# Half-row sections of an attention kernel's TensorE stream also hold the queries' last products and half of the diagonal key tile

## The reference, cut to what matters

```python
q_nop = (c_Q @ Wq_up)            # 16 heads x 128
q_pe  = rope(c_Q @ Wq_pe)        # 16 heads x 64
scores = einsum(q, k) * SCALE    # q = [q_nop, q_pe], k = [k_nop, k_pe]
scores = where(tril, scores, min)
attn = softmax(scores); y = attn @ v; out = y @ Wo
```

## Time and profile before

| what | value |
|---|---|
| median of 3 runs | 1749.84 us (1749.19 to 1750.82) |
| the profiled execution, own time | 1748.17 us |
| its span in the trace | 1746.1 us |
| TensorE clock granted, mean | 0.992 of full speed |
| attention starts (first of the units' stream) | 106.0 us |
| PE, DVE, ACT, POOL busy | 97%, 76%, 65%, 33% of the span |

### The profile page before, as it was taken

How to read it: one execution, slowest core, us unless ns; L and a number is a source line. 1 busy time by engine, 2 the same in 40 slices (tenths; PEclk the granted TensorE clock), 3 DMA queues, 4 the chain that set the end, 5 groups by cost and what they waited for, 6 DMA issues and landing times.

```text
span 1746.1 us, 29372 instructions
## 1 busy us (share of the span) xinstructions
PE 1688.8 (97%) x9224; PEld 852.3 (49%) x9224; DVE 1332.8 (76%) x3370; ACT 1135.1 (65%) x2464; POOL 583.5 (33%) x1042
## 2 busy tenths in 40 slices
PE   4589999999999999999999999999999999999999
PEld 3345545454544545544454455555454454554444
DVE  5688787777778787787868788777878878777775
ACT  5677666666666666666667566666766666666663
POOL 1223333333333333433333333333333333333330
PEclk9899999999999999999999999999999999999999
DMA  9338977878979787886879978887797888897786
GB/s 267 83 70 146 152 138 146 147 143 153 153 129 151 152 148 149 154 154 123 154 135 155 173 136 148 143 148 132 150 159 141 154 145 147 150 152 145 138 152 129
DMA packets 911877, 255.05 MB, mean 146 GB/s; under 512 B 897384, under 2 KB 899946, under 8 KB 911338
## 3 DMA queue, kind: packets, MB, share of 16 engines
q1 hardware_dynamic: 902336, 235.29, 75.7%
q10 hardware_dynamic: 8938, 15.80, 3.1%
q0 software_dynamic: 448, 2.10, 0.5%
HBM read 20.32 MB, written 8.39 MB: 16 GB/s over the span
## 4 chain that ended last, share of the span: by engine, by line
PE 85%; DVE 4%; issue 4%; ACT 3%; DMA 2%; POOL 1%; SPq 1%; ACTq 0%; DVEq 0%; POOLq 0%
PE bank L623 7%; PE bank L591 7%; PE bank L593 7%; PE bank L594 7%; PE bank L592 7%; PE bank L625 6%; PE bank L624 6%; PE bank L657 6%; PE bank L659 6%; PE bank L658 6%; PE bank L603 3%; DMA XT<-XS 2%; PE bank L596 2%; PE bank L397 2%; PE bank L398 1%
## 5 line engine op out<-in xcount | busy, mean ns | idle before, releaser
L924 ACT ACTIVATE P<-P,nm 128x512 f32<-128x512 f32 (+7 forms) x512 | 395.0, 772 | 459.6 <-DVE nm L1332 457.6
L1332 DVE CUSTOM_DVE_ANT_0 P<-bank,mask,neg 128x512 f32<-128x512 f32 (+7 forms) x512 | 402.5, 814 | 280.2 <-PE bank L603 167.7
L1554 POOL TENSOR_SCALAR sn<-sm 128x1 f32<-128x1 f32 x512 | 206.8, 405 | 944.8 <-ACT P L924 935.1
L919 ACT ACTIVATE F<-P,rc 128x512 f16<-128x512 f32 (+7 forms) x512 | 384.8, 767 | 85.2 <-DVE rc L1340 65.4
L1346 DVE SCALAR_TENSOR_TENSOR F<-P,rc,F 128x512 f16<-128x512 f32 (+7 forms) x512 | 413.3, 819 | 2.8 <-ACT F L919 2.4
L592 PE MATMUL bank<-K,Q 128*128 128x512 f16 (+3 forms) x760 | 248.5, 327 | 0.0
L594 PE MATMUL bank<-K,Q 128*128 128x512 f16 (+3 forms) x760 | 248.5, 327 | 0.0
L591 PE MATMUL bank<-K,Q 128*128 128x512 f16 (+3 forms) x760 | 248.5, 327 | 0.0
L593 PE MATMUL bank<-K,Q 128*128 128x512 f16 (+3 forms) x760 | 248.5, 327 | 0.0
L623 PE MATMUL bank<-FT,V 128*128 128x512 f16 x568 | 216.7, 382 | 3.3 <-DVE WO L1381 3.3
L624 PE MATMUL bank<-FT,V 128*128 128x512 f16 x568 | 215.5, 379 | 0.0
(11 more groups left out here) (211 smaller groups left out, 2675.8 us busy)
## 6 DMA issues: line engine op xcount, KB each, us to landing
out<-X ACTq DMA_DIRECT2D x31, 256.0 KB, 3.5
X<-in_x ACTq DMA_DIRECT2D x28, 256.0 KB, 3.6
FT<-F SPq DMA_TRANSPOSE x348, 4.2
wo<-in_Wo SPq DMA_DIRECT2D x4, 1024.0 KB, 9.0
V<-CC SPq DMA_DIRECT2D x32, 64.0 KB, 2.4
Q<-QS SPq DMA_TRANSPOSE x128, 4.0
X<-in_x SPq DMA_DIRECT2D x4, 256.0 KB, 7.4
ua<-in_Wq_up SPq DMA_DIRECT2D x1, 1024.0 KB, 8.6
```

What stands on the lines that cost most here:

```text
L919: return e.eng.activation(dst, src, ACT.Copy, scale=scale)
L924: e.eng.activation(m.P[:, u % 4, 0:w], m.P[:, u % 4, 0:w], ACT.Exp, bias=m.nm[:, u % 8:u % 8 + 1], scale=-1.0, accum_out=m.sm[:, u % 8:u % ...
L1332: e.eng.tensor_tensor_reduce(out=m.P[:, u % 4, 0:w], in0=m.pS[u % 2][:, off:off + w], in1=m.mask[:, 1024 - w:1024], scale=m.neg[:, :], sca ...
```

## The change

`sections(n)` gives two truth values for unit n: whether the half-row section of quarter 0 and that of quarter 2 are widened. The second is true for all n below 124; the first where the tile of unit n + 2 has i >= 2 besides, and n is not `late`. `halved(n, p)` now says for each pair of heads whether its fifth products are done in halves: for i >= 4 as before (that test is now called `wide`), and for every pair that stands ahead of a widened section, so also for i below 4.

Quarter 0, where widened: behind the two half-row score products comes `up_pe_half(n + 4)`, rows 64 to 127 of `lb` against the high weights, 256 columns, then `diagonal_half`: for the diagonal key tile, queries 0 to 63 of each head against keys 0 to 63 alone (rows 0 to 63), high x high, 256 columns; then `diagonal_rest`, queries 64 to 127 against all 128 keys, in all rows, 256 columns. Keys 64 to 127 are masked for queries 0 to 63, so that nothing is left out there.

Quarter 2, where widened: `up_half(n + 4)`, 512 columns in rows 64 to 127; `diagonal_half` for the other two products of the diagonal, 2 x 256 columns in rows 0 to 63; `diagonal_rest` for these, 2 x 256 columns in all rows. If the unit's quarter 0 was not widened, the diagonal's high x high product follows whole (512 columns).

So `up` and `up_pe` have four full products left instead of five, and `weigh` runs over j = 0 to i - 1 alone, cut anew into quarters (k = i instead of i + 1). For i = 0 no weighing is left outside quarter 2. The waits move along: those of `up_pe` and `up` to ahead of the half products, that of the first weighing (`weigh_ready`) to the first part of the diagonal where quarter 0 is widened or i = 0. The weights' halves change places (high parts in rows 64 to 127), the copies that write them keep their shapes. The half products leave out low x low of the 64 channels.

The diff, cut to its core (`up_pe` and `up_pe_half` are changed as `up` and `up_half` are; the remaining lines exchange the halves of the weights or rename `halved` to `wide`):

```diff
@@ -52,9 +52,22 @@
     JBASE.append(JBASE[-1] + where(_n)[1] + 1)
 
 
+def sections(n):
+
+
+
+    both = n + 2 * AHEAD < N
+    return both and where(n + AHEAD)[1] >= 2 and not late(n), both
+
+
+def halved(n, p):
+
+    return wide(where(n)[1]) or sections(n - AHEAD)[p]
+
+
 def quarter(n, q):
 
-    k = where(n)[1] + 1
+    k = where(n)[1] + (not sections(n)[1])
     return range(-(-k * q // 4), -(-k * (q + 1) // 4))
 
 
...
@@ -406,23 +419,34 @@
     def __init__(self, e, m, s):
         self.e, self.m, self.s = e, m, s
 
-    def up(self, n):
-        e, m, s = self.e, self.m, self.s
-        t, g = divmod(n, NG)
+    def up_ready(self, n):
+        e, s = self.e, self.s
         if n >= NG:
             e.wait_ge(s.ropeq, n + 1)
         elif n:
             e.wait_ge(s.ql, n)
+
+    def up_half(self, n):
+
+        m, (t, g) = self.m, divmod(n, NG)
+        self.up_ready(n)
+        self.e.eng.matmul(m.pU, m.C[64:128, t % 2, 3, :], m.WM[64:128, g, WMB:WMB + 512], start=True, stop=False)
+
+    def up(self, n, begun=False):
+        e, m, s = self.e, self.m, self.s
+        t, g = divmod(n, NG)
+        self.up_ready(n)
         W = m.WM[:, g, :]
         hq, hb, lq, lb = (m.C[:, t % 2, k, :] for k in range(4))
-        e.eng.matmul(m.pU, hq, W[:, WMA:WMA + 512], start=True, stop=False)
+        e.eng.matmul(m.pU, hq, W[:, WMA:WMA + 512], start=not begun, stop=False)
+        if not begun:
+            e.eng.matmul(m.pU, lb, W[:, WMB:WMB + 512], start=False, stop=False)
         e.eng.matmul(m.pU, hq, W[:, WMA + 512:WMA + 1024], start=False, stop=False)
         e.eng.matmul(m.pU, lq, W[:, WMA:WMA + 512], start=False, stop=False)
-        e.eng.matmul(m.pU, hb, W[:, WMB:WMB + 512], start=False, stop=False)
-        e.eng.matmul(m.pU, lb, W[:, WMB:WMB + 512], start=False, stop=True).then_inc(s.up, 1)
-
-    def up_pe(self, n):
-        e, m, s = self.e, self.m, self.s
+        e.eng.matmul(m.pU, hb, W[:, WMB:WMB + 512], start=False, stop=True).then_inc(s.up, 1)
+
+    def up_pe_ready(self, n):
+        e, s = self.e, self.s
         t, g = divmod(n, NG)
         e.wait_ge(s.c_in, 16 * (t + 1))
         e.wait_ge(s.wpl, 2 * min(n + 1, NG))
...
@@ -592,11 +629,11 @@
                 e.eng.matmul(o, Q[:, h, :], K[:, ALO, keys], start=False, stop=False)
                 e.eng.matmul(o, Q[:, 4 + h, :], K[:, AHI, keys], start=False, stop=False)
                 e.eng.matmul(o, Q[:, 8 + h, :], K[:, BHI, keys], start=False, stop=False)
-                if not halved(i):
+                if not halved(n, p):
                     op = e.eng.matmul(o, Q[:, 8 + h, :], K[:, BLO, keys], start=False, stop=True)
-            if not halved(i):
+            if not halved(n, p):
                 op.then_inc(s.s, 1)
-        if halved(i):
+        if halved(n, p):
             for lo, hi in cuts:
                 for h, top in ((2 * p, 0), (2 * p + 1, 64)):
                     o, keys = m.pS[h % 2][:, off + lo:off + hi], slice(base + lo, base + hi)
@@ -604,25 +641,64 @@
                     if hi == cuts[-1][1]:
                         op.then_inc(s.s, 1)
 
-    def weigh(n, j):
-        b, i, g = where(n)
+    downs = ffns = 0
+
+    def weigh_ready(n):
+
         for z in range(GROUP_OF[4 * n], GROUP_OF[4 * n + 3] + 1):
             e.wait_ge(s.ft_in[z % FSLOTS], 16 * (z // FSLOTS + 1))
         e.wait_ge(s.v_in, 16 * (n // NG + 1))
         if n >= 2:
             e.wait_ge(s.yl, n - 1)
-        if j == 0 and n:
-            e.wait_ge(s.cr, tiles.downs)
-            e.wait_ge(s.od, tiles.ffns)
-        elif j == 0:
+        if n:
+            e.wait_ge(s.cr, downs)
+            e.wait_ge(s.od, ffns)
+        else:
             e.wait_ge(s.wol, 16)
+
+    def weighed(n, j, lo, hi):
+
+
+        b, i, g = where(n)
         ft = turned_at(m, n, 0, 1024 * (i + 1)).rearrange("p (h c q) -> p h c q", h=4, q=128)
-        hi, lo = ft[:, :, j, :], ft[:, :, i + 1 + j, :]
-        o = m.pY[n % 2].rearrange("p (h q) -> p h q", h=4)
         V = m.V[:, key_slot(b, j), :, :]
-        e.eng.matmul(o, V[:, 0, :], hi, start=(j == 0), stop=False)
-        e.eng.matmul(o, V[:, 0, :], lo, start=False, stop=False)
-        e.eng.matmul(o, V[:, 1, :], hi, start=False, stop=(j == i)).then_inc(s.pv, 1)
+        o = m.pY[n % 2].rearrange("p (h q) -> p h q", h=4)[:, :, lo:hi]
+        return o, V[:, 0, :], V[:, 1, :], ft[:, :, j, lo:hi], ft[:, :, i + 1 + j, lo:hi]
+
+    def weigh(n, j, start=False, stop=False):
+        o, vh, vl, hi, lo = weighed(n, j, 0, 128)
+        if start:
+            weigh_ready(n)
+        e.eng.matmul(o, vh, hi, start=start, stop=False)
+        e.eng.matmul(o, vh, lo, start=False, stop=False)
+        e.eng.matmul(o, vl, hi, start=False, stop=stop).then_inc(s.pv, 1)
+
+    def diagonal_half(n, first, start=False):
+
+
+        o, vh, vl, hi, lo = weighed(n, where(n)[1], 0, 64)
+        if start:
+            weigh_ready(n)
+        if first:
+            e.eng.matmul(o, vh[0:64], hi[0:64], start=start, stop=False)
+        else:
+            e.eng.matmul(o, vh[0:64], lo[0:64], start=start, stop=False)
+            e.eng.matmul(o, vl[0:64], hi[0:64], start=False, stop=False)
+
+    def diagonal_rest(n, first, stop=False):
+
+        o, vh, vl, hi, lo = weighed(n, where(n)[1], 64, 128)
+        if first:
+            op = e.eng.matmul(o, vh, hi, start=False, stop=stop)
+        else:
+            e.eng.matmul(o, vh, lo, start=False, stop=False)
+            op = e.eng.matmul(o, vl, hi, start=False, stop=stop)
+        return op
+
+    def diagonal_whole(n, stop=False):
+
+        o, vh, vl, hi, lo = weighed(n, where(n)[1], 0, 128)
+        return e.eng.matmul(o, vh, hi, start=False, stop=stop)
 
     def weigh_pair(p):
 
@@ -669,24 +745,41 @@
             tiles.down(2, m.pO)
     for n in range(N - 1):
         t, g = divmod(n, NG)
+        first, second = sections(n)
+        k = where(n)[1] + (not second)
+        done = 0
+        downs, ffns = tiles.downs, tiles.ffns
         for q in range(4):
             if q % 2 == 0 and n + AHEAD < N:
                 pair(n + AHEAD, q // 2)
+            if q == 0 and first:
+                queries.up_pe_half(n + 2 * AHEAD)
+                diagonal_half(n, True, start=True)
+                diagonal_rest(n, True)
             if q == 0 and late(n):
                 queries.up_pe(n + 2 * AHEAD)
                 combine(n - 1, 0)
+            if q == 2 and second:
+                queries.up_half(n + 2 * AHEAD)
+                diagonal_half(n, False, not first and done == 0)
+                op = diagonal_rest(n, False, first and done == k)
+                if not first:
+                    op = diagonal_whole(n, done == k)
+                op.then_inc(s.pv, 1)
             for j in quarter(n, q):
-                weigh(n, j)
+                done += 1
+                weigh(n, j, not first and j == 0, done == k and (q >= 2 or not second))
             if q == 0 and n + 2 * AHEAD < N and not late(n):
-                queries.up_pe(n + 2 * AHEAD)
+                queries.up_pe(n + 2 * AHEAD, first)
             if q == 1 and (g == 3 and t + LEAD < T or g == 0 and t + LEAD - 1 < T):
                 e.wait_ge(s.yl, n)
+                e.wait_ge(s.wol, 16)
                 if g:
                     tiles.down(t + LEAD, m.pY[(n + 1) % 2])
                 else:
                     tiles.ffn(t + LEAD - 1, m.pY[(n + 1) % 2])
             if q == 2 and n + 2 * AHEAD < N:
-                queries.up(n + 2 * AHEAD)
+                queries.up(n + 2 * AHEAD, second)
             if q % 2 and n and n + AHEAD < N and not (q == 1 and late(n)):
                 combine(n - 1, q // 2)
     combine(N - 3, 0)
...
@@ -831,17 +924,17 @@
         e.wait_ge(s.wm, 2 * k + 1)
         copy(W[:, WMA:WMA + 512], fold_bank(m, k, 3), m.sq[:, 0:1]).then_inc(s.wph, 1)
         e.wait_ge(s.wm, 2 * k + 2)
-        copy(W[0:64, WMB:WMB + 512], fold_bank(m, k, 4)[0:64, :], m.sq[0:64, 1:2]).then_inc(s.wph, 1)
+        copy(W[64:128, WMB:WMB + 512], fold_bank(m, k, 4)[64:128, :], m.sq[64:128, 1:2]).then_inc(s.wph, 1)
         if k:
             e.wait_ge(s.wpl, 2 * k)
-        copy(m.tmp[64:128, :], fold_bank(m, k, 4)[64:128, :], m.sq[64:128, 1:2]).then_inc(s.wph, 1)
+        copy(m.tmp[0:64, :], fold_bank(m, k, 4)[0:64, :], m.sq[0:64, 1:2]).then_inc(s.wph, 1)
 
     def rotary_out():
         e.wait_ge(s.ld_pb, 32)
         e.wait_ge(s.sc, 1)
         copy(m.WM[:, :, WQA:WQA + 256], m.pa[:, :, :], m.sqp[:, 0:1]).then_inc(s.wrh, 1)
-        copy(m.WM[0:64, :, WQB:WQB + 256], m.pbw[0:64, :, :], m.sqp[0:64, 1:2]).then_inc(s.wrh, 1)
```

More of the change, by code:

```diff
@@ L108, in score_cuts, with wide @@
     return off, [(0, cut)] + ([(cut, w)] if w > cut else [])
-def halved(i):
+def wide(i):
     return i >= 4
 def early(n):
-    return halved(where(n)[1]) and (n == N - 1 or not halved(where(n + 1)[1]))
+    return wide(where(n)[1]) and (n == N - 1 or not wide(where(n + 1)[1]))
 def late(n):
@@ L435, in up_pe, with up_pe_half @@
```

(32 more changed lines are left out.)

## The result

The changed kernel runs in 1737.94 us (median of 4 runs, 1737.78 to 1739.36), the kernel before in 1750.06 (4 runs, 1749.19 to 1750.82): ratio 0.9933, 95% interval 0.9915 to 0.995. Forecast were 1740.8 us and 9.0 us less; it became 12.1 less (by the interval 8.8 to 14.9 us, which holds the forecast).

The account below looks back on a forecast made before the run. PE, busy 97%, was taken as the bound, with only 0.28 us to spare before waiting for DVE. 30.0 us saved less 21.0 given back left 9.0: 1749.84 - 9.0 = 1740.8 us, range 1728 to 1756.

Parts of the forecast that it names:

- other such places: Unspecified places like the one between index 5 and 0, where PE may wait: 1.5 us given back.
- PE's side: Slots saved on PE: 8.8 us in quarter 0, 25.3 in quarter 2, less 4.1 for new low-index sections; 30.0 in all.
- fixed 0.20 of a section: Each half-row section on PE costs 0.20 us once: 0.09 to enter, 0.09 to leave, 0.01 a pair.
- new sections in low tiles: Pairs of heads with index below 4 get a half-row section they lacked: 4.1 us lost on PE in sum.
- Unequal halves: Quarter 2: forecast took full overlap; the rival said no overlap as pairs, 13.6 us back, 1754.4, slower, chance 0.12.
- Waits behind late masks: PE waits for YL behind later masks; index 2: combine at 4.30 us, waits 0.83, 0.83 and 0.6, 6.6 + 3.6 us.
- Index 0: Key tile moves from quarter 0 to behind the wait for YL: 5.0 us given back, window some 0.4 longer.
- Index 4 to 7: Tiles where DVE has several us to spare: nothing given back, windows shorter by 0.8 to 1.2 us.
- index 1: PE already waits at ffn, so savings ahead are lost and later masks add 0.2: 0.5 a tile, 2.0 us.
- Between index 5 and 0: up_half, asked two key tiles earlier than up, meets DVE's rotation: 0.5 us three times, 1.5 given back.
- waits for DMAs: No DMA added, moved or passed; the wait for XT on PE booked at 0.

Follow-up runs that it names:

- e7: Changed kernel with the diagonal's half products moved to rows 64 to 127, where the queries' halves run: 1770.19 us, ratio 1.0114 to the kernel before.
- e1: Changed kernel with the key tiles cut into quarters as in the kernel before: 1729.56 us, ratio 0.9878 to the kernel before.
- e2: Changed kernel with YL put ahead of the masks on DVE wherever quarter 0 is widened: 1725.48 us, ratio 0.9855 to the kernel before.
- e5: Changed kernel with quarter 2 not widened in the first two units of each index 0 tile: 1735.41 us, ratio 0.9915 to the kernel before.
- e6: Changed kernel with quarter 0 widened only where the scores have index 4 or more: 1734.62 us, ratio 0.9909 to the kernel before.
- e10: Changed kernel with the diagonal's half product issued ahead of up_pe_half in quarter 0: 1736.58 us, ratio 0.992 to the kernel before.
- e4: Changed kernel with fifth products kept whole, per head, for pairs of heads below index 4: 1738.29 us, ratio 0.9932 to the kernel before.
- e8: Changed kernel with YL ahead of the masks in all units not late, and index 0's first two units without widened quarter 2: 1722.10 us, ratio 0.9841.

## Why the prediction was right

It was right in sign and mechanism, and in size within the interval: fewer slots on PE, some 60% of them given back, most of it to waits for YL behind late masks. The two sums were 30.0 us saved and 21.0 given back; the traces have 30.6 and 18.4, by the tiles' index, in us over all four sequences:

| index | slots saved | given back | forecast of that |
|---|---|---|---|
| 0 | 2.6 | 3.7 | 5.0 |
| 1 | 3.2 | 1.3 | 3.2 |
| 2 | 4.3 | 9.6 | 9.0 |
| 3 | 5.1 | 0.9 | 0.8 |
| 4 | 5.1 | 0.0 | 0 |
| 5 | 3.5 | 0.9 | 1.5 |
| 6 and 7 | 6.9 | 2.1 | 1.5 ("other such places") |
| all | 30.6 | 18.4 | 21.0 |

- *PE's side.* Forecast: 0.097 us a section in quarter 0, 0.204 in quarter 2, together 0.301 a unit with index 4 and more. Measured: 56.66 - 55.38 = 1.28 a tile with index 4, 0.32 a unit: a further pair costs its slot and nothing beside, where I had booked 0.01 for each. The fixed 0.20 of a section held, but the first product behind it takes 0.01 more, which makes the new sections in low tiles dearer than booked; the two nearly cancel.
- *Unequal halves* overlap fully (L433 with L685 and L686 above), which I had taken without a row; e7 shows what it would have been otherwise. On the rule of the Trainium skill (TensorE: Matmul & The Clock Gate, Part 3) that matmuls end in the program's order: L685 is issued behind L433, is listed ahead of it and ends at 845.86 by the record, ahead of its 845.97 (ends are modelled, so this does not refute the rule); and L686 starts 0.11 us in, when half of L433's slot is still to come. Whatever order the ends keep, it holds up nothing in other rows.
- *Waits behind late masks.* Forecast for index 2: `combine` at 4.30, measured 4.34; the tile longer by 1 to 1.5, measured 1.31; e1 and e2 removed it in two ways that leave the sections alone. The list of waits rose further than forecast, to 17.1 us instead of some 10. I had read 3.1 us there before, and it was 4.2. The longest, 1.1 us, is in the second unit of a tile with index 0, not in index 2.
- *Index 0:* 0.4 longer forecast, 0.44 measured, cause shown by e5.
- *Index 4 to 7* shorter by 0.8 to 1.2, it said: index 4 by 1.28, but index 7 only by 0.60 and index 6 by 0.75 and less (the last tile with index 6, which no low tile follows, by 1.28). Of index 7's shortfall the third unit is the larger part: the prediction has no term for `up_pe_half` waiting for `ql` there, but it did wait (0.21 us), and the diagonal queued behind it (e6, e10). In index 6 it is the third unit too, 0.27 us longer instead of shorter; the old cut of the key tiles takes that away (e1).
- *Too dear:* index 1, where I let the units' whole savings be lost (forecast, from the sum, about 0.3 less a tile; measured 46.70 to 46.02, 0.67).
- *Between index 5 and 0* I had priced the wait for the rotation alone, at 0.5. It is 0.30 us, but in the same unit `combine` now waits 0.61 us for YL instead of 0.16, so that this unit is 0.70 longer. The late unit after it is 1.06 us shorter in the second sequence and 0.90 in the third, since PE no longer waits there for XT (0.83 and 0.74 us before), and 0.50 longer in the first, where it waits for XT and FT.

This last point is luck. The prediction put the waits for DMAs at 0; in the stream they went from 2.9 to 1.7 us between these two traces, and in other runs the same unit of the same sequence waits between 0 and 1.7 us. So about 1.2 of the 3.1 us by which the change did better than forecast need no other cause. The rest is 0.6 us of slots, and index 0 and 1, which were priced too dear.

Open: the tiles that differ by up to 2.3 us between runs of kernels that do the same in them (the first sequence's index 1, those with index 5 and 6) do so by PE's waits for XT and FT; why these transfers come at other times is not shown. No run tried e4's edit on e8. In e8 `combine` still waits for YL in the last two units of the first three tiles with index 5 (0.61 and 0.40 us), and no run tried to remove that. Nor was e2's edit run on the kernel before, so what the order is worth there isn't measured; the 4.2 us of listed waits for YL suggest that it is much less.

## What to carry to other kernels

A busy share of 97% says that one engine's slots are the currency, but not that a saved slot is paid out: before shortening an engine's stream, list for each of its waits how long the awaited thing has been there, and look at what shrinks below zero. The cheapest cure for such a wait is order: an instruction that is free to run, put on the awaited engine into the idle time it has anyway (e2), or on the waiting engine into the wait (e1). Here the change alone gained 12 us, and these cures on top of it 16 more (e8), mostly by taking away waits that the change had made.

## What the runs showed of the hardware that I had not expected

- A half-row product in free rows doesn't get past one that waits. If it has semaphores of its own, they are taken only then: with `up_pe_half` held, the diagonal's half started 0.21 us after it in spite of its data being there (e10). Without any, it starts together with the one that waited (776.11 above). So where such products have waits of their own, the one with the later data belongs last.
- Two short half products run one after the other beside a long one (0.11 us apart, L685 and L686) at no cost: the halves need not be equally long, as long as the columns in each half of the rows add up to the same, 512 here.
- Entering and leaving half rows cost 0.10 us each whether 2 (e4) or 7 half products stood between.
